# The joint last stage: an own order for its filling, and another order and engine for its last steps

## What is computed

```
L2:  h = layernorm(x);  q = h Wq (16 heads of 64);  k, v = ctx Wk, ctx Wv
     x = x + (softmax(q k^T) / sqrt(64) @ v) Wo + bo
L3:  q = x Wq (16 heads of 8);  k, v = ctx Wk, ctx Wv
     x = x + (softmax(q k^T / sqrt(8)) @ v) Wo + bo
```

## Time and profile before

| | |
|---|---|
| median of the runs | 1671.55 us (1671.17 to 1672.45, 3 runs) |
| profiled execution | 1667.4 us |
| span of its instructions | 1665.6 us |
| TensorE busy over the span | 1599.6 us, 96% |
| VectorE, ScalarE, GpSimd busy | 1201.9, 1046.6, 756.7 us |
| the last stage | from 1104.2 us to the end of the span |

### The profile page before, as it was taken

One profiled execution on the slowest core, in us unless ns is written; L12 is line 12 of the kernel. 1 busy time (PEld: TensorE's weight loads), 2 busy tenths in 40 slices (PEclk: granted clock), 3 DMA queues, 4 the chain that ended last, 5 costly groups with the idle time before them and its releaser, 6 DMA issues. The chain is left out here.

```text
span 1665.6 us, 49749 instructions
## 1 busy us (share of the span) xinstructions
PE 1599.6 (96%) x18240; PEld 1365.4 (82%) x18240; DVE 1201.9 (72%) x2395; ACT 1046.6 (63%) x3075; POOL 756.7 (45%) x1126
## 2 busy tenths in 40 slices
PE   7999999999999999989999998978999999999997
PEld 6888888878888888868978887867898898898986
DVE  5777777777777777746757775646887787888872
ACT  4777777777777777743336665435666666666663
POOL 3444444454444444422314442644555554555541
PEclk9999999999999999999999999998999999999997
DMA  7777667788677767740040000004545446444430
GB/s 198 197 196 188 184 184 200 201 210 217 185 187 192 188 185 192 190 140 9 0 115 2 3 3 2 1 1 127 154 137 166 145 136 178 124 141 146 135 117 9
DMA packets 229002, 220.07 MB, mean 132 GB/s; under 512 B 20610, under 2 KB 225092, under 8 KB 228740
## 3 DMA queue, kind: packets, MB, share of 16 engines
q1 hardware_dynamic: 228836, 217.79, 47.5%
HBM read 116.01 MB, written 101.71 MB: 131 GB/s over the span
## 5 line engine op out<-in xcount | busy, mean ns | idle before, releaser
L952 POOL TENSOR_TENSOR L_probs<-L_probs,L_inv_sum 128x1024 f32<-128x1024 f32 x128 | 242.8, 1897 | 88.3 <-DVE L_inv_sum L848 88.3
L736 ACT ACTIVATE L_probs<-L_scores,L_neg_max 128x128 f32<-128x128 f32 x512 | 182.7, 386 | 134.6 <-DVE L_neg_max L828 134.6
L822 DVE TENSOR_REDUCE L_row_max<-L_scores 128x8 f32<-128x1024 f32 x128 | 156.2, 1220 | 42.5 <-PE L_scores L594 42.5
L854 DVE STREAM_TRANSPOSE L_squares<-L_probs 128x1024 f32<-128x1024 f32 x125 | 153.0, 1224 | 0.3 <-POOL L_probs L952 0.3
L1983 POOL TENSOR_TENSOR L2L_w_probs<-L2L_w_probs,L2L_w_inv_sum 128x1024 f32<-128x1024 f32 x64 | 121.4, 1896 | 62.0 <-DVE L2L_w_inv_sum L1863 60.4
L1999 POOL TENSOR_SCALAR L2L_n_k_apart<-L2L_n_qk,quad_mask 128x128 f32<-128x128 f32 x128 | 55.5, 448 | 186.1 <-ACT L2L_n_qk L1724 175.8
L1735 ACT ACTIVATE L2L_w_probs<-L2L_scores,L2L_w_neg_max 128x128 f32<-128x128 f32 x256 | 91.2, 385 | 74.3 <-DVE L2L_w_neg_max L1843 74.3
L594 PE MATMUL L_scores<-L_kT,L_qT 64*128 64x128 f32 x2048 | 131.8, 278 | 0.9 <-ACT L_kT L725 0.9
L645 PE MATMUL L_ring<-L_probsT,L_v 128*64 128x128 f32 x2048 | 126.6, 276 | 4.7 <-issue 3.8
L645 PEld LDWEIGHTS L_ring<-L_probsT,L_v 128*64 128x64 f32 x2048 | 110.5, 137 | 24.7 <-issue 21.8
L594 PEld LDWEIGHTS L_scores<-L_kT,L_qT 64*128 64x128 f32 x2048 | 119.4, 188 | 12.5 <-ACT L_oT L725 8.1
(11 more groups left out here) (239 smaller groups left out, 4491.7 us busy)
## 6 DMA issues: line engine op xcount, KB each, us to landing
L_relay<-L_squares SPq DMA_DIRECT2D x125, 512.0 KB, 3.4
L_probsT<-L_relay SPq DMA_DIRECT2D x500, 128.0 KB, 3.7
L2L_relay<-L2L_w_squares SPq DMA_DIRECT2D x62, 512.0 KB, 3.6
L2L_w_probsT<-L2L_relay SPq DMA_DIRECT2D x248, 128.0 KB, 2.9
ctx_blocks<-ctx_turned SPq DMA_DIRECT2D x48, 128.0 KB, 3.5
out_x<-x SPq DMA_DIRECT2D x32, 64.0 KB, 2.8
ctx_turned<-ctxT SPq DMA_DIRECT2D x1, 1536.0 KB, 7.1
L0a_wq<-in_L_xattn_Wq SPq DMA_DIRECT2D x2, 256.0 KB, 3.1
```

The source lines that it names most:

```text
L736: done = nc.scalar.activation(slot_probs(at, 0)[:, n, :], scores[:, 0, r, i, :], ACT.Exp, scale=layer_of(at).scale, bias=neg_max[:, n:n + ...
L822: nc.vector.tensor_reduce(row_max[:, s, :], slot(s), AX.X, ALU.max).then_inc(max_ready[s], 1)
L854: nc.vector.transpose(squares[:, at.n % 2, :, SLOT_HEADS * s:SLOT_HEADS * (s + 1), :] .rearrange("p j h a -> p h j a"), slot_probs(at, s). ...
L952: nc.gpsimd.tensor_tensor(to, to, inv_sum[:, :, s, :].unsqueeze(3) .to_broadcast([TOKENS, 2, GROUP, TOKENS]), ALU.mult).then_inc(divided, 1)
```

## The change

The loop starts at t = 0, and what steps -4 to -1 did is written out ahead of it for each engine, with an order of fills of its own (`filled_before`). TensorE makes the keys of the first pair first, then turns batches 0 and 1, makes the queries of batch 0, its scores, the queries of batch 1, turns batch 2 and makes the values of batch 0. The ten products for the clock are gone. VectorE normalises batches 0, 1 and 2, which GpSimd did, and clears the two tiles after this work, right ahead of the loop. In the loop the inverse deviation on GpSimd gets a wait for the normalising of two batches before.

At the end: the parts of the last batch are made by VectorE, at the end of step 32 (`n_set_last_parts`); in step 33 VectorE divides batch 29 after the first maxima of batch 31, and TensorE turns batch 29 back between the two passes of scores; in step 34 the shifted scores of batch 31 are made in one pass of all four groups, groups 0 and 1 in the first slot's banks, and batch 30 is turned back after it.

```diff
-    first, last = -4, BATCHES + 3
+    first, last = 0, BATCHES + 3
+    DVE_NORMALISES = 3
+    kv = [(f"w.kv{g}", "dve" if g == 1 else "act") for g in QUARTERS]
+    filled_before = [*((name, -2, engine) for name, engine in kv), ("w.hT", 0, "dve"), ("w.hT", 1, "dve"),
+                     ("w.q0", 0, "act"), ("w.q1", 0, "act"), ("w.q0", 1, "act"), ("w.q1", 1, "act"),
+                     ("w.hT", 2, "dve"), *((name, -1, engine) for name, engine in kv)]
...
-        def t_bank(g):
-            return scores[:, 1, g % 2, :, :]
+        def t_bank(b, g):
+            return scores[:, 0 if b == BATCHES - 1 and g < 2 else 1, g % 2, :, :]
...
-            keep_clock(nc, scores[:, 0, 0, 0, :], ident, START_COUNT)
...
-                    if g < 2:
+                    if g < 2 and b == BATCHES - 1:
+                        pe.wait_ge(n_max_ready, 4 * b + 4)
+                    elif g < 2:
                         pe.wait_ge(n_exp_ready, 4 * b + g + 1)
...
+            w_keys(-2)
+            for b in range(2):
+                w_transpose_h(b)
+            for n in range(2):
+                w_queries(0, n)
+            for s in range(2):
+                w_score(0, s)
+            for n in range(2):
+                w_queries(1, n)
+            w_transpose_h(2)
+            w_values(-1)
             for t in range(first, last + 1):
...
-                if real(t - 4):
+                if real(t - 4) and t not in (LAST_WIDE + 2, LAST_WIDE + 3):
                     n_turn_back(t - 4)
-                n_both_scores(t, (0, 1), (2, 3))
+                if t == LAST_WIDE + 3:
+                    n_both_scores(t, (), (2, 3, 0, 1))
+                else:
+                    n_both_scores(t, (0, 1), (2, 3))
...
-                n_both_scores(t, (2, 3), (0, 1))
+                if t == LAST_WIDE + 2:
+                    n_turn_back(t - 4)
+                if t != LAST_WIDE + 3:
+                    n_both_scores(t, (2, 3), (0, 1))
+                if t == LAST_WIDE + 3:
+                    n_turn_back(t - 4)
...
+            w_keys_values(-2, (0, 2, 3))
+            w_queries(0, 0)
+            w_queries(0, 1)
+            w_queries(1, 0)
+            w_exponentiate_0(0, 0)
+            w_queries(1, 1)
+            w_exponentiate_0(0, 1)
+            w_keys_values(-1, (0, 2, 3))
+            w_exponentiate_1(0)
...
+            w_statistics(0)
+            w_statistics(1)
+            w_normalise(0)
+            w_keys_values(-2, 1)
+            w_turned_h(0)
+            w_normalise(1)
+            w_statistics(2)
+            w_turned_h(1)
+            w_row_maxima(0, 0)
+            w_negate_maxima(0)
+            w_row_maxima(0, 1)
+            w_subtract_maxima(0)
+            w_normalise(2)
+            w_turned_h(2)
+            w_invert(0, 0)
+            w_statistics(3)
+            w_keys_values(-1, 1)
+            w_turn_squares(0, 0)
+            nc.vector.memset(n_maxima[:, :, :, :, :], 0.0).then_inc(cleared, 1)
+            nc.vector.memset(n_v[:, :, :, :, :], 0.0).then_inc(cleared, 1)
+            dve.wait_ge(cleared, 2)
+            nc.vector.memset(n_v[:, :, :, :, NARROW:NARROW + 1], 1.0).then_inc(cleared, 1)
...
+            def n_set_last_parts():
+                b = LAST_WIDE
+                await_emptied(dve, "n.qk", b)
+                dve.wait_ge(n_t_full, 4 * (b - 2) + 4)
+                dve.wait_ge(n_parts_ready, b)
...
-                if real(t - 4):
+                if real(t - 4) and t != LAST_WIDE + 2:
                     n_divide(t - 4)
...
+                if t == LAST_WIDE + 2:
+                    n_divide(t - 4)
...
+                if t == LAST_WIDE + 1:
+                    n_set_last_parts()
...
                 pool.wait_ge(moments_ready, b + 1)
+                if b >= 2:
+                    pool.wait_ge(w_rows_h_ready, b - 1)
...
+            for b in range(DVE_NORMALISES):
+                w_inverse_deviation(b)
             nc.gpsimd.memset(no_bias[:, :], 0.0).then_inc(masks_ready, 1)
...
+            w_divide(0, 0)
+            w_inverse_deviation(3)
             for t in range(first, last + 1):
-                if real(t - 2):
+                if real(t - 2) and t - 2 != LAST_WIDE:
                     n_set_parts(t - 2)
...
+            away(0, 0)
+            back(0, 0)
             for t in range(first, last + 2):
```

More of the change, by code:

```diff
@@ L1342, in values_made @@
         return (b + 1) // 2 * 2 - 1
-    ring = Fills((name, t + lag, engine) for t in range(first, last + 1)
-                 for name, lag, engine in (turned_by_pe if t == LAST_WIDE + 1 else []) + order
-                 if (makes_keys_values(t) if name.startswith("w.kv") else 0 <= t + lag < BATCHES))
+    ring = Fills(filled_before + [(name, t + lag, engine) for t in range(first, last + 1)
+                                  for name, lag, engine in (turned_by_pe if t == LAST_WIDE + 1 else []) + order
+                                  if (makes_keys_values(t) if name.startswith("w.kv") else 0 <= t + lag < BATCHES)])
     chunks = INNER // 128
@@ L1524, in n_score_less_max @@
                         pe.wait_ge(n_exp_ready, 4 * b - 3 + g)
-                last = nc.tensor.matmul(t_bank(g)[:, j, :], n_k_apart[part, b % 2, j, :],
+                last = nc.tensor.matmul(t_bank(b, g)[:, j, :], n_k_apart[part, b % 2, j, :],
                                         n_q_part[part, b % 2, j // 2, :],
@@ L1745, in n_exponentiate @@
                 nc.scalar.activation(n_exps[:, b % 2, GROUP * g:GROUP * (g + 1), :].rearrange("p h q -> p (h q)"),
-                                     t_bank(g).rearrange("p j q -> p (j q)"), ACT.Exp,
+                                     t_bank(b, g).rearrange("p j q -> p (j q)"), ACT.Exp,
                                      scale=N.scale).then_inc(n_exp_ready, 1)
@@ L1817, in _ @@
                 dve.wait_ge(semaphore, value)
[L1818 to L1821, removed]
             def slot_scores(s):
@@ L1833, in w_statistics, with w_normalise @@
                 nc.vector.bn_aggr(moments[:, p, :], stats[:, p, :]).then_inc(moments_ready, 1)
+            def w_normalise(b):
+                dve.wait_ge(moments_ready, b + 1)
+                dve.wait_ge(rstd_ready, b + 1)
+                if b >= 1:
+                    await_filled(dve, "w.hT", b - 1)
+                nc.vector.tensor_scalar(w_rows_h[:, :], x[:, b, :], moments[:, b % 2, 0:1], rstd[:, b % 2, :],
+                                        ALU.subtract, ALU.mult).then_inc(w_rows_h_ready, 1)
             def w_row_maxima(b, s):
@@ L1900, in n_append_maxima @@
                                                n_q_part[:, b % 2, 1, :], ALU.mult, ALU.add).then_inc(emptied["dve"], 1)
+            def n_set_last_parts():
[3 more added lines that the diff above has]
+                dve.wait_ge(n_parts_ready, b)
+                for j in range(GROUP):
+                    other = (j + 2) % GROUP
+                    nc.vector.tensor_scalar(n_k_apart[:, b % 2, j, :], n_qk[:, b % 2, 1, :], quad_mask[:, j:j + 1],
+                                            quad_mask[:, other:other + 1], ALU.mult, ALU.add)
+                for n in range(2):
+                    done = nc.vector.tensor_scalar(n_q_part[:, b % 2, n, :], n_qk[:, b % 2, 0, :],
+                                                   half_mask[:, n:n + 1], no_bias[:, :], ALU.mult, ALU.add)
+                done.then_inc(n_parts_ready, 1)
             def n_divide(b):
```

## The result

The changed kernel takes 1653.66 us (median of 5 runs, 1650.31 to 1657.83) against 1671.17 for the kernel before in the same comparison (1663.95 to 1672.45). The ratio is 0.9914 with an interval of 0.989 to 0.9938: faster by 0.6 to 1.1%. The forecast was 1661.4 and its range ended at 1657.1, so the change brought more than the range allowed. Of the runs further down, one of warm_drain_old (1786.7 us) lay far above all others and is left out of its ratio. The profiled execution took 1651.88 us with a span of 1650.2, against 1667.4 and 1665.6.

The account below looks back on a forecast made before the run. TensorE's own work bounds the loop, so only fill and drain count: 7.8 + 2.4 = 10.2 us off the profiled 1667.4 gives 1657.2, plus 4.15 carried over to the runs' median gives 1661.4. Range 1657.1 to 1667.7.

Parts of the forecast that it names:

- The fill step: Start of the last stage up to the loop: keys first and the new order save 7.8 us, between 4.9 and 9.5.
- Row maximum of batch 1: Fill, on VectorE: starts at 1123.7 instead of 1131.50, 7.8 us earlier, directly behind the memsets.
- the uncovered clearing: Fill, on VectorE ahead of the loop: clearing two tiles costs 2.0 us, hidden by nothing, before batch 1's row maximum.
- the point named as a warning: Fill: the prediction called itself wrong if the first exponentials came later than 1115.
- the upper bound of 9.5: Fill: largest gain, if the 1.7 us lost at half rate over 1142.1 to 1145.5 stay away too.
- Rival A: Clock takes half the fill's gain back after TensorE's idle time, keys losing 2.87; total gain 4.6, 1667.0 us; chance 0.20.
- Rival D: Loop meets more half-rate stretches of 1.7 us each and the kernel is slower; ten give 1678 us; chance 0.04.
- The drain's order: End of the stage: parts on VectorE and one pass weigh batch 31 2.6 us earlier; 2.4 taken.
- the pass of 32: Drain, on TensorE: batch 31's shifted scores in one pass, taken as 1.8 us, bounds 1.16 and 4.9.
- The parts: Drain: last batch's parts made by VectorE instead of GpSimd, between 0 and 0.6 us earlier, 0.6 taken.
- B: Drain brings nothing: the single pass runs at half rate, 4.9 us; total gain 7.3, 1664.3 us; chance 0.12.
- The low end of the range: Whole kernel: fill 9.5, drain 3.2 and one loop stretch of 1.7 less, 14.4 us gained, 1657.1 us.

Follow-up runs that it names:

- warm_drain_old: Changed kernel with the drain of before put back, plus products in TensorE's drain waits serving only its clock; 0.9902 of the kernel before.
- clear_early: Changed kernel with the clearing of the two tiles moved into VectorE's idle time ahead of batch 0's row maximum; 0.9904 of the kernel before.
- warm_fill: Changed kernel with 20 products for the clock ahead of the keys of step 0; 0.9914 of the kernel before.
- parts_only: Changed kernel with two passes of last scores and old places of turning back and division; last parts stay on VectorE; 0.9957 of the kernel before.
- early_warm: Changed kernel with tile clearing moved into VectorE's earlier idle time and clock products in the drain's TensorE waits; 1649.31 us.

## Why the prediction was wrong

**The fill step was right.** Keys first for 2.87: 2.87. Scores of batch 0 at 1111.4: 1111.68. Row maximum of batch 1 at 1123.7, directly behind the clearing: 1124.25, or 7.75 earlier counted from the stage's start, against 7.8. The 2.0 for the uncovered clearing were 2.03 (clear_early). The first exponential came at 1115.36, 0.36 later than the point named as a warning, and cost nothing that shows. The rest of the fill's 8.71 is the scores of batch 2, which took 2.97 at half rate before and 2.06 after: the gain that the upper bound of 9.5 had in it.

**Rival A, the clock taking back half of the fill, was half right in its mechanism.** TensorE did stand idle for 6.61 us, and the keys did run at half rate. The price was 0.54 us at most and not 2.87, because of the cover that the prediction named (VectorE's squares); warm_fill shows it. The removed warm-up shows no price: the first keys took 2.87, the full rate, in every kernel with the new fill. The rule that was weighed there (the Trainium skill, "TensorE: Matmul & The Clock Gate", Part 1: the throttled state is the default, activity releases it) agrees with the keys at half rate behind the idle time.

**Rival D read its row as half rate without a cause in TensorE.** It took 1398.0 to 1401.5 for a fall with TensorE busy throughout. TensorE was busy there, but the stretch starts right behind 2.07 us of waiting for a transfer, which rows 1 don't show. So this fall goes with a wait. The wait alone doesn't make it: behind 2.04 us of the same wait the changed kernel kept 1.00.

**The drain's order was a little undersized.** Taken at 2.4 out of a worked 2.6, bounds -0.5 to 3.2; at one rate it is 2.8 to 3.0. The mis-sized term is the pass of 32: taken as 1.8, it took 1.17, its lower bound. The parts were 0.63 to 0.65, taken as 0.6. There the row decided rightly against the Trainium skill ("GPSIMD Engine Reference", section 4.1: one-input operations at about line rate), by which the exchange would have brought little: the same six operations take 2.6 on GpSimd and 1.6 on VectorE.

**The step that failed: the drain's clock was carried over as it was.** The prediction took every duration of the old drain as it stood in the profile, with the weighing of batch 30 at 1.93 (it was 1.08), and asked only whether the new pass would run at half rate (rivals A and B). It read the clock as a risk. But the old drain had 6.8 us at 0.50 between the first scores of batch 31 and the end of the weighing of batch 30, and more behind it; at full rate it would be 19.79 by warm_drain_old, and it took 23.74. So some 4 us of the kernel before were a loss that a new order could give back, and 2.7 to 2.9 of the 5.69 came from there. The low end of the range held one loop stretch of 1.7 for such returns, and none for the drain. The profiled gain of 15.5 lies 1.1 beyond the 14.4 that the range allowed; without the drain's 2.7 it would lie within. In the fill the same carrying over did no harm: the old fill's half-rate groups came again in every profile that has it (keys 4.36, 4.52 and 4.48; fills 45.10, 45.28 and 46.14).

**What was chance.** The loop's 1.55: among kernels with the same loop it took from 486.65 to 491.47, and 494.20 once. In it TensorE waits up to three times for probabilities to come back from DRAM (1.0 to 7.6 us in all), and in eight of the 14 profiles the clock fell to 0.50 within 1.2 us of the end of such a wait. So the loop is not quite without idle time, as the prediction had it. Also the base: the prediction carried over the 4.15 us by which the median of the three runs shown lay above the profiled run. That carry-over is a second step that failed: the three runs had 1671.55, but the 8, 11 and 19 runs of the later comparisons have 1667.8 to 1669.4. For the changed kernel that distance was 1.8 (1653.66 against 1651.88). So of the 7.7 us by which the forecast missed, 5.3 are in the sum (fill 0.9, loop 1.55, drain 3.3, start -0.5) and 2.4 in the base.

**What stays open.** Why the clock fell in the old drain, and not in the new one ahead of the weighing, is not shown. Shorter waits are not the answer: up to its fall at 1643.8 no wait of the old drain was longer than 0.49 us, and the new one has waits of 0.78 and 0.52 (in the lines above) without a fall; its own fall comes at the weighing of batch 31, behind 0.71. The last wait before the fall, and the whole way from the turning of batch 30's maxima to the weighing of batch 31, before:

```profile
1643.91 1.39 PE L1509 MATMUL L2L_scores<-L2L_n_k_apart,L2L_n_q_part 32*128 32x256 f32 x3 [0.39 <-DVE L2L_n_maxima L1891]
```

```profile
1638.77:1657.88 19.11, 15.39 (x163) 11.88 (x161) 5.61 (x15) 6.43 (x17) 3.48 (x8) 0.72 0.03 8
```

and after:

```profile
1629.01:1642.41 13.40, 9.81 (x162) 7.24 (x161) 7.03 (x21) 6.42 (x17) 0.91 (x2) 1.00 0.04 12
```

TensorE was idle for 3.72 us before and 3.59 after. Products put into the old drain's waits kept the rate up; that, and the fall ahead of the weighing in three of four old drains and in none of eight new ones, is all the runs show.

## What to carry to other kernels

Before costing an edit in a stretch with a clock below 1.00, work out what the stretch would take at the full rate: the difference is neither safe nor lost, and belongs into the range on the side of gain as well as of loss. An idle time and a half-rate group behind it cost only what no other engine covers; look for what the next consumer waits for before warming anything up. Two small passes with a wait between them are worth joining when banks can be had: here 2.2 us at equal rate (7.30 against 5.12).

## What the runs showed of the hardware

- A pass of 32 matmul instructions (16 products) of 32 rows over four row groups took 1.17 us at the full rate, as long as 16 instructions on two groups (1.16): twice the row groups cost no time here.
- Earlier stages with the same code and order end at different times: the stage started between 1102.97 and 1108.35 us in 14 profiles. Apart from the one run left out, runs of one kernel scatter by 5 to 11 us, and the median of the three runs of before that stood at the start was some 3 us above that of 19.
- In the loop the granted clock fell from 1.00 to 0.50 ten times, in eight of 14 profiles, within 1.2 us of the end of waits of 2.00 to 3.25 us for a transfer; TensorE then was busy at half rate. Behind 2.04 us (after) and 2.39 (warm_drain_old) it did not fall. The longest loop, 494.20 us in warm_fill, has two such falls and 7.6 us of these waits, against 4.4 in the changed kernel.
- Elsewhere it fell behind shorter waits: in the drain of the kernel before none up to the fall was above 0.49 us, and late in the loops of parts_only and early_warm the two waits before a fall were 0.71 and 0.26, and 0.74 and 0.26 us.
